# Attention and router block on one Trainium2 core: zero products ahead of the first weights' products, the first four weight combinations in four PSUM banks, and a new order of the opening

## The chip, the cores and the metric

One core of a Trainium2 chip. The metric is the time on the device in microseconds (us), the median of several runs of one launch.

## What is computed

```python
x = hidden_states                                    # (4, 512, 512), fp32
mod = (silu(c) @ wmod).reshape(4, 6, 1, 512)         # sa, ca, ga, sb, cb, gb
h = layernorm(x) * (1 + ca) + sa
# attention: 32 heads of 128, 8 kv heads, causal
q = rope(h @ Wq.T)
k = concat(h @ Wdk.T @ Wupk.T, rope(h @ Wkr.T))      # 64 + 64 of the 128 columns
v = h @ Wdk.T @ Wupv.T
x = x + ga * (softmax(q k.T / sqrt(128)) @ v @ Wo.T)
h = layernorm(x) * (1 + cb) + sb
# router: softmax over 64 experts, top 8, weighted bias rows
x = x + gb * (h * sum(top8) + top8_weights @ expert_bias)
```

The gates ga and gb are kept at least 0.25 from zero.

## The kernel before, in words

Every matrix is split into a high part in fp32r and a low part (the value less the high part), and each product is three: high by high, high by low, low by high (`passes`). The main loop `step(t)` goes over 128 heads (8 kv groups, 4 batches, 4 heads of a group); ahead of it stands an opening of some 100 us, whose order on each engine is written out by hand. Engines meet through counting semaphores.

The opening has these pieces. The names in brackets are helpers of the engines' programs:

- **Combined weights.** Wup times Wdk, once for all batches: `combine(i)`, i from 0 to 15, on PE (L606 to L614). i // 4 is one of four pieces of Wup, i % 4 a slice of 128 columns of Wdk. A combination is 12 products of 384 columns, into the bank of COMBINE_BANKS. ACT copies each to wc_out and counts act_comb (L1063), SP stores it to HBM. The first needs the split of wup (ACT L1060, DVE L1459) and of wdk in four pieces (ACT L1054, DVE L1454).
- **Modulation.** `modulation(j)`, j = 0 and 1: 16 fp32 products from c_silu and wmod (L566), transposed by `transpose_modulation` (L580) in bank pv and copied by DVE to modT.
- **h.** For batch b: DVE's `statistics`, POOL's `statistics` (rstd and shift_x), ACT's `normalise_x(b)` (four instructions on y, L1072), PE's `transpose_h(n)` (4 transposes; n // 4 is the batch), DVE's `modulate_h(n)`, ACT's `split_h(n)` and POOL's `split_h(n)` for high and low part. transpose_h(n) waits for act_xn, normalise_x of its batch.
- **First weights.** SP's `load_first(i)` brings wq0, wk, wq1, wv, wq2, wq3 in turn into two stage buffers; ACT's `split_first(i)` makes the high part, POOL's `split_piece` the low one. wk comes in two loads, of which the second reads the stored combinations back, so SP waits there until the first four are stored.
- **Heads.** `k_proj(0)`, `q_proj(t)` (12 products of 512 columns each), then DVE's and POOL's rope (rot_c, rot_s, kv_rot), ACT's and POOL's `q_split` and `k_split`, and `scores(t)`. q_proj(t) for t under 5 writes bank pv and waits until DVE's `q_rope(t - 1)` (L1467 to L1469) has read the one before. DVE's q_rope(t) waits for POOL's q_split(t - 1), because rot_c is one buffer.

The order on PE: combinations 0, 1, 2, modulation 0, combination 3, modulation 1, transpose_h 0 and 1, transpose_modulation, and so on (L903 to L940). SP has one queue for all loads and stores.

```python
def transpose_h(n):
    b, c = n // CH, n % CH
    pe.wait_ge(act_xn, b + 1)
...
def q_proj(t):
...
    elif t > 0:
        pe.wait_ge(dve_r, t)
```

## Time and profile before

| what | us |
|---|---|
| median of 3 runs | 1451.87 (1451.16 to 1452.57) |
| the profiled execution | 1451.52 |
| its span, first to last instruction | 1450.2 |
| PE busy | 1430.0 (99%) |
| DVE, ACT, POOL busy | 1152.9, 1009.4, 1023.5 |
| PE's first product | at 9.28 |

The page gives shares over the whole span. For the opening one reads the timeline, which lists the instructions of each engine by start, with the idle time before and what ended it. The ends of matmuls are modelled, so their distance from start to start says more than their duration. The span leaves out 1.3 us that lie around it.

### The profile page before, as it was taken

How to read it: one execution, taken by the hardware profiler on the slowest of the kernel's cores; microseconds unless marked ns; L12 is line 12 of the kernel's file. 1: busy time of each engine (PE TensorE's matmuls, PEld its weight loads, DVE VectorE, ACT ScalarE, POOL GpSimd, SP SyncE). 2: the span in 40 equal slices, each digit the busy share in tenths (PEclk: the TensorE clock that was granted, in tenths of full speed). 3: DMA queues.
4: the chain of work that ended last, by engine and by line, in shares of the span. 5: the costliest groups of instructions: out<-in, count | busy, mean ns of one | idle time of the engine just before them, and what ended most of it. 6: DMA issues, size and time to landing. Idle time of an engine off the chain costs nothing.

```text
span 1450.2 us, 24714 instructions
## 1 busy us (share of the span) xinstructions
PE 1430.0 (99%) x7150; PEld 1209.0 (83%) x7150; DVE 1152.9 (79%) x3542; ACT 1009.4 (70%) x2391; POOL 1023.5 (71%) x805
## 2 busy tenths in 40 slices
PE   7999999999999999999999999999999999999998
PEld 7888888888888888888888888888888888888886
DVE  6697777777777777778777777777879989888876
ACT  5687767667767667676777677676667676776674
POOL 3777777667767666776666677667588887887662
PEclk9999999999999999999999999999999999999999
DMA  9488658766766866686588668659888889888972
GB/s 316 157 248 255 213 179 229 221 213 184 213 202 199 228 197 214 191 244 180 172 229 241 203 180 227 181 176 259 241 229 267 264 284 272 277 256 271 269 234 68
DMA packets 215158, 322.05 MB, mean 222 GB/s; under 512 B 42512, under 2 KB 132464, under 8 KB 215024
## 3 DMA queue, kind: packets, MB, share of 16 engines
q1 hardware_dynamic: 214736, 320.39, 74.2%
q8 instruction: 59, 0.97, 0.3%
q14 instruction: 75, 0.61, 0.1%
q10 hardware_dynamic: 288, 0.07, 0.0%
HBM read 179.43 MB, written 140.95 MB: 221 GB/s over the span
## 4 chain that ended last, share of the span: by engine, by line
PE 90%; DVE 4%; DMA 2%; issue 1%; POOL 1%; ACT 1%; SPq 0%; DVEq 0%; ACTq 0%
PE bank_s L642 22%; PE bank_o L804 22%; PE bank_pv L766 14%; PE bank_s L708 13%; PE bank_s L674 6%; PE bank_s L659 5%; PE bank_s L613 2%; DMA PT_raw<-blocks 1%; PE bank_pv L642 1%; PE bank_s L704 1%; PE bank_o L613 1%; POOL PT_lo L1891 1%; PE bank_s L868 1%; DVE blocks L1529 0%; DMA blocks<-blocks 0%
## 5 line engine op out<-in xcount | busy, mean ns | idle before, releaser
L1891 POOL TENSOR_TENSOR PT_lo<-PT_raw,PT_hi 128x640 fp32r<-128x640 f32 x246 | 382.7, 1577 | 30.7 <-ACT PT_hi L1152 30.7
L1138 ACT ACTIVATE probs<-probs,row_inv 128x512 f32<-128x512 f32 (+3 forms) x512 | 257.7, 553 | 193.7 <-DVE row_inv L1512 193.6
L1879 POOL TENSOR_TENSOR rot_c<-rot_c,rot_s 128x512 f32<-128x512 f32 x128 | 167.9, 1312 | 251.7 <-DVE rot_s L1469 251.7
L1131 ACT ACTIVATE probs<-probs,row_min 128x384 f32<-128x384 f32 (+3 forms) x512 | 281.6, 552 | 47.2 <-DVE row_min L1505 47.1
L1529 DVE STREAM_TRANSPOSE blocks<-probs 128x384 f32<-128x384 f32 x508 | 213.9, 447 | 19.7 <-ACT probs L1138 13.5
L708 PE MATMUL bank_s<-kT_both,qT_hi 128*128 128x512 f32 (+2 forms) x768 | 215.5, 341 | 1.8 <-issue 1.1
L1505 DVE CUSTOM_DVE_ANT_0 probs<-bank_s,mask 128x512 f32<-128x512 f32 (+2 forms) x384 | 205.3, 552 | 0.3
L1884 POOL TENSOR_TENSOR qT_lo<-rot_c,qT_hi 128x512 fp32r<-128x512 f32 x128 | 166.3, 1299 | 51.4 <-ACT qT_hi L1113 50.6
L804 PE MATMUL bank_o<-wo_lo,OT_hi 128*128 128x512 f32 x496 | 195.0, 393 | 0.4 <-DVE rot_s L1469 0.4
L804 PE MATMUL bank_o<-wo_hi,OT_hi 128*128 128x512 f32 x496 | 193.4, 390 | 0.0
L642 PE MATMUL bank_s<-hT_lo,wq_hi 128*128 128x512 f32 x480 | 193.0, 402 | 0.4
L804 PE MATMUL bank_o<-wo_hi,OT_lo 128*128 128x512 f32 x496 | 193.0, 389 | 0.0
L642 PE MATMUL bank_s<-hT_hi,wq_hi 128*128 128x512 f32 x480 | 188.5, 393 | 0.0
L642 PE MATMUL bank_s<-hT_hi,wq_lo 128*128 128x512 f32 x480 | 187.4, 390 | 0.0
L1152 ACT ACTIVATE PT_hi<-PT_raw 128x640 fp32r<-128x640 f32 x250 | 169.9, 728 | 17.3 <-DMA PT_raw<-blocks 17.2
L708 PEld LDWEIGHTS bank_s<-kT_both,qT_hi 128*128 128x128 f32 x768 | 142.5, 188 | 19.3 <-issue 3.1
L1467 DVE TENSOR_TENSOR rot_c<-bank_s,cos_t 128x512 f32<-128x512 f32 x120 | 82.8, 690 | 81.0 <-PE bank_s L642 80.2
L1545 DVE TENSOR_TENSOR OT_lo<-bank_pv,OT_hi 128x512 fp32r<-128x512 f32 x123 | 84.6, 688 | 78.5 <-ACT OT_hi L1162 78.5
L766 PE MATMUL bank_pv<-PT_lo,v_hi 128*128 128x512 f32 x372 | 135.3, 369 | 1.3 <-DVE OT_lo L1545 0.8
L766 PE MATMUL bank_pv<-PT_hi,v_lo 128*128 128x512 f32 x372 | 132.5, 356 | 0.3 <-DVE OT_lo L1545 0.3
L766 PE MATMUL bank_pv<-PT_hi,v_hi 128*128 128x512 f32 x372 | 132.0, 356 | 0.0
L708 PE MATMUL bank_s<-kT_both,qT_lo 128*128 128x512 f32 (+2 forms) x384 | 129.2, 337 | 0.0
(311 smaller groups left out, 3198.0 us busy)
## 6 DMA issues: line engine op xcount, KB each, us to landing
blocks<-blocks SPq DMA_DIRECT2D x127, 640.0 KB, 3.6
PT_raw<-blocks SPq DMA_DIRECT2D x500, 160.0 KB, 3.9
stage<-in_wq SPq DMA_DIRECT2D x32, 256.0 KB, 5.2
vblocks<-kv_raw SPq DMA_DIRECT2D x32, 256.0 KB, 5.4
kv_raw<-vblocks SPq DMA_DIRECT2D x128, 64.0 KB, 2.2
stage<-in_wo SPq DMA_DIRECT2D x32, 256.0 KB, 5.1
split_wq<-wq_hi SPq DMA_DIRECT2D x32, 256.0 KB, 5.4
split_wq<-wq_lo SPq DMA_DIRECT2D x32, 256.0 KB, 5.8
```

The source lines that it names most:

```text
L642: mm = pe.matmul(q_bank(t)[:], w[:, h, c, :], x[:, b * CH + c, :], start=(c == 0 and n == 0), stop=(c == CH - 1 and n == 2))
L708: mm = pe.matmul(score_bank[qt], q, k[:, 0:keys], start=(n == 0), stop=(n == 2))
L766: mm = pe.matmul(to[:, :, (first - tiles[0]) * SUB:], v_part[:, kb, :], ps[:, :, at:at + size], start=(start and kb == 0 and n == which[0] ...
L804: mm = pe.matmul(bank[f"o{j}"][:], o[:, o_at:o_at + P], w[:, h, :], start=(u < LAST_UNIT and h == 0 and n == 0), stop=(u < LAST_UNIT - 1 a ...
L1131: ins = act.activation(row(t, qt), row(t, qt), ACT.Exp, bias=row_min[m][:, qt:qt + 1], scale=-1.0, accum_out=row_sum[m][:, qt:qt + 1])
L1138: ins = act.activation(row(t, qt), row(t, qt), ACT.Copy, scale=row_inv[t % 2][:, qt:qt + 1])
L1152: act.activation(parts_of(t)[0][:, at], raw_of(t)[:, at], ACT.Copy).then_inc(act_t, 1)
L1505: dve.tensor_tensor_reduce(row(t, qt), score_bank[qt], row(t, 0) if qt == 0 else mask[:, SEQ - (qt + 1) * P:], -SCALE, -LOWEST, ALU.add, A ...
L1529: ins = dve.transpose(blocks_v[:, qt:qt + 3 * whole_keys - 2:3], keys[:, 0:whole_keys])
L1879: pool.tensor_tensor(rot_c[:], rot_c[:], rot_s[:], ALU.add).then_inc(pool_a, 1)
L1884: pool.tensor_tensor(lo[:], rot_c[:], hi[:].bitcast(F32), ALU.subtract).then_inc(pool_q, 1)
L1891: pool.tensor_tensor(lo[:, at], raw_of(t)[:, at], hi[:, at].bitcast(F32), ALU.subtract).then_inc(pool_t, 1)
```

## The change

1. **Zero products.** WARM_UPS = 13 fp32 products of 128 columns from kv_rot, into bank s1, where nobody reads them. DVE clears kv_rot as its first instruction for that (before, it did so ahead of the split).
2. **Splits piece by piece.** wup's first piece is split in four pieces in turn with wdk's four (`split_first_weights` on ACT and DVE), in place of one whole wup and four of wdk.
3. **Side by side.** `combine_first` makes combinations 0 to 3 together in banks s3, s2, pv and o3: for each of the four pieces, first the four products of high by high, then the 32 with a low part, one combination after the other. The number of products is the same. transpose_modulation and k_proj(0) wait for ACT's copies out of pv and o3.
4. **Order.** On PE, modulation 0 follows combination 3, and the later combinations move among the transposes; combination 10 goes from behind transpose_h(7) to ahead of k_proj(0). On ACT, normalise_x(0) goes behind combinations 2 and 3, and normalise_x(1) behind split_first(1). On POOL, split_h(1) goes ahead of statistics(1) and k_split(0) ahead of split_h(6). On DVE, modulate_h(1) goes ahead of statistics(1). On SP, the load of wmod[1] goes ahead of the first store.

```diff
-COMBINE_BANKS = ["s3", "s2"] * (SOON // 2) + ["o0", "o1"] * ((COMBINED - SOON) // 2)
+SIDE_BY_SIDE = ["s3", "s2", "pv", "o3"]
+COMBINE_BANKS = SIDE_BY_SIDE + ["s3", "s2"] * ((SOON - CH) // 2) + ["o0", "o1"] * ((COMBINED - SOON) // 2)
+WARM_UPS = 13
...
-        SILU, POWER, ROT_CLEAR, HALF, MODT = 5, 6, 7, 8, 9
+        ROT_CLEAR, SILU, POWER, HALF, MODT = 1, 6, 7, 8, 9
...
                 pe.wait_ge(d_ident, 16)
+                pe.wait_ge(act_comb, SIDE_BY_SIDE.index("pv") + 1)
...
+            def warm_up():
+
+                pe.wait_ge(dve_pro, ROT_CLEAR)
+                for _ in range(WARM_UPS):
+                    pe.matmul(bank["s1"][:, 0:P], kv_rot[:, 0:P], kv_rot[:, P:2 * P], start=True, stop=True)
+
+            def combine_first():
+
+                for m in range(CH):
+                    pe.wait_ge(split_w, 2 * m + 2)
+                    for i in range(CH):
+                        pe.matmul(bank[COMBINE_BANKS[i]][:, 0:2 * KVC], wdk[0][:, m, i * P:(i + 1) * P],
+                                  wup_hi[0][:, m, :], start=(m == 0), stop=False)
+                for i in range(CH):
+                    for m in range(CH):
+                        if i == 0:
+                            pe.wait_ge(split_lo, 2 * m + 2)
+                        for k, (down, up) in enumerate(((wdk[0], wup_lo[0]), (wdk[1], wup_hi[0]))):
+                            mm = pe.matmul(bank[COMBINE_BANKS[i]][:, 0:2 * KVC], down[:, m, i * P:(i + 1) * P],
+                                           up[:, m, :], start=False, stop=(m == CH - 1 and k == 1))
+                    mm.then_inc(pe_comb, 1)
+
             def combine(i):
                 n, c = i // CH, i % CH
                 ps = bank[COMBINE_BANKS[i]]
                 if c == 0:
-                    pe.wait_ge(split_lo, n + 1 + (CH if n > 0 else 0))
-                if i >= 2:
-                    pe.wait_ge(act_comb, i - 1)
+                    pe.wait_ge(split_lo, n + 2 * CH)
+                pe.wait_ge(act_comb, i - 3 if i < CH + 2 else i - 1)
                 for m in range(CH):
-                    if i == 0:
-                        pe.wait_ge(split_lo, m + 2)
...
-            combine(0)
-            combine(1)
-            combine(2)
+            warm_up()
+            combine_first()
             modulation(0)
-            combine(3)
+            combine(4)
             modulation(1)
             transpose_h(0)
             transpose_h(1)
             transpose_modulation()
-            combine(4)
             combine(5)
             transpose_h(2)
             combine(6)
             transpose_h(3)
             combine(7)
             combine(8)
+            combine(9)
             transpose_h(4)
             transpose_h(5)
-            combine(9)
+            combine(10)
             pe.wait_ge(pool_h, CH)
+            pe.wait_ge(act_comb, SIDE_BY_SIDE.index("o3") + 1)
             k_proj(0)
             transpose_h(6)
             pe.wait_ge(pool_h, CH)
             pe.wait_ge(dve_pro, MODT)
             q_proj(0)
             transpose_h(7)
-            combine(10)
             q_proj(1)
             combine(11)
...
-            def split_down():
+            def split_first_weights():
+                act.wait_ge(d_wup[0], 16)
                 for m in range(CH):
+                    act.activation(wup_hi[0][:, m, :], wup_in[0][:, m, :], ACT.Copy).then_inc(split_w, 1)
                     act.wait_ge(d_wdk[m], 16)
...
-            split_up(0)
-            split_down()
+            split_first_weights()
             combine(0)
             split_up(1)
             combine(1)
-            normalise_x(0)
             combine(2)
             combine(3)
+            normalise_x(0)
+            combine(4)
             split_h(0)
-            combine(4)
+            split_h(1)
             split_up(2)
+            combine(5)
             split_first(0)
-            combine(5)
-            split_h(1)
+            combine(6)
             split_h(2)
-            combine(6)
-            normalise_x(1)
             split_h(3)
             combine(7)
             split_first(1)
+            normalise_x(1)
             combine(8)
             split_first(2)
             split_h(4)
             combine(9)
             split_h(5)
+            combine(10)
             normalise_x(2)
             split_up(3)
+            k_split(0)
             split_h(6)
-            k_split(0)
             split_first(3)
+            q_split(0)
             split_first(4)
-            combine(10)
-            q_split(0)
             split_h(7)
+            q_split(1)
             combine(11)
-            q_split(1)
...
-            def split_down():
+            def split_first_weights():
                 for m in range(CH):
-                    dve.wait_ge(split_w, m + 2)
+                    dve.wait_ge(split_w, 2 * m + 1)
+                    dve.tensor_tensor(wup_lo[0][:, m, :], wup_in[0][:, m, :], wup_hi[0][:, m, :].bitcast(F32),
+                                      ALU.subtract).then_inc(split_lo, 1)
+                    dve.wait_ge(split_w, 2 * m + 2)
...
+            dve.memset(kv_rot[:], 0.0).then_inc(dve_pro, 1)
             dve.memset(c_silu[:], 0.0).then_inc(dve_pro, 1)
             dve.wait_ge(act_pro, 1)
             dve.tensor_scalar(c_exp[:], c_exp[:], 1.0, None, ALU.add).then_inc(dve_pro, 1)
-            dve.wait_ge(dve_pro, 2)
+            dve.wait_ge(dve_pro, 3)
             dve.reciprocal(c_exp[:], c_exp[:]).then_inc(dve_pro, 1)
-            dve.wait_ge(dve_pro, 3)
+            dve.wait_ge(dve_pro, 4)
             dve.tensor_tensor(c_keep[:], c_in[:], c_exp[:], ALU.mult).then_inc(dve_pro, 1)
-            dve.wait_ge(dve_pro, 4)
+            dve.wait_ge(dve_pro, 5)
             dve.tensor_copy(c_silu[:, :, 0:BATCH], c_keep[:]).then_inc(dve_pro, 1)
             dve.memset(power[:], -0.5).then_inc(dve_pro, 1)
-            dve.memset(kv_rot[:], 0.0).then_inc(dve_pro, 1)
             dve.memset(minus_half[:], -0.5).then_inc(dve_pro, 1)
-            split_up(0)
-            split_down()
+            split_first_weights()
             statistics(0)
             split_up(1)
             keep_modulation(0)
             keep_modulation(1)
             transpose_modulation()
             modulate_h(0)
+            modulate_h(1)
             statistics(1)
-            modulate_h(1)
...
             statistics(0)
             split_h(0)
+            split_h(1)
             statistics(1)
             split_piece(FIRST_CHUNKS[0], 0, 0)
-            split_h(1)
             split_h(2)
             split_h(3)
             split_piece(FIRST_CHUNKS[1], 1, 1)
...
             split_h(4)
             split_h(5)
             k_rope(0)
+            k_split(0)
             split_h(6)
             q_rope(0)
-            k_split(0)
...
+            sp.dma_start(wmod[1][:], wmod_v[MOD_PIECES[1]]).then_inc(d_wmod[1], 16)
             store_combined(0)
-            sp.dma_start(wmod[1][:], wmod_v[MOD_PIECES[1]]).then_inc(d_wmod[1], 16)
```

ACT from its first exponential on: before, and then after. The names are wup and wdk (weights to combine) and wc_out (a combination's copy).

```order
L1271 ACTIVATE c_exp<-c_in 128x16
L1060 ACTIVATE wup_hi_171<-wup_in_173 128x1536
L1054 ACTIVATE wdk_hi<-wdk_in 128x512 x4
L1066 ACTIVATE wc_out_177<-bank_s 128x384
L1060 ACTIVATE wup_hi_172<-wup_in_175 128x1536
```

```order
L1294 ACTIVATE c_exp<-c_in 128x16
L1075 ACTIVATE wup_hi_171<-wup_in_173 128x384
L1077 ACTIVATE wdk_hi<-wdk_in 128x512
L1075 ACTIVATE wup_hi_171<-wup_in_173 128x384
L1077 ACTIVATE wdk_hi<-wdk_in 128x512
L1075 ACTIVATE wup_hi_171<-wup_in_173 128x384
```

The one long split of wup became four, each followed by a piece of wdk; the last two pairs stand below the rows shown.

ACT between the copy of combination 6 and the second piece of wq, before and after. `y<-y` is normalise_x(1), `wk_hi` is split_first(1), `hT_hi` is split_h.

```order
L1066 ACTIVATE wc_out_178<-bank_s 128x384
L1079 ACTIVATE hT_hi<-h_raw 128x512 x2
L1066 ACTIVATE wc_out_179<-bank_s 128x384
L1072 ACTIVATE y<-y,shift_x,rstd 128x512 x4
L1079 ACTIVATE hT_hi<-h_raw 128x512
L1066 ACTIVATE wc_out_180<-bank_s 128x384
L1092 ACTIVATE wk_hi<-stage_58 128x512
L1066 ACTIVATE wc_out_177<-bank_s 128x384
```

```order
L1089 ACTIVATE wc_out_179<-bank_s 128x384
L1102 ACTIVATE hT_hi<-h_raw 128x512 x2
L1089 ACTIVATE wc_out_180<-bank_s 128x384
L1115 ACTIVATE wk_hi<-stage_58 128x512
L1095 ACTIVATE y<-y,shift_x,rstd 128x512 x4
L1089 ACTIVATE wc_out_177<-bank_s 128x384
L1115 ACTIVATE wq_hi<-stage_57 128x512
L1102 ACTIVATE hT_hi<-h_raw 128x512
```

The four instructions on y stood ahead of wk_hi and now stand behind it.

PE from the end of q_proj(0) to the start of what follows transpose_h(7), before and after. `bank_pv` is a head's projection, `ident,y` a transpose.

```order
L642 MATMUL bank_pv<-hT_hi,wq_lo 128x512
L642 MATMUL bank_pv<-hT_hi,wq_hi 128x512
L599 MATMUL bank_o<-ident,y 128x128 x4
L613 MATMUL bank_o<-wup_lo_174,wdk_hi 128x384
L613 MATMUL bank_o<-wup_hi_171,wdk_lo 128x384
L613 MATMUL bank_o<-wup_hi_171,wdk_hi 128x384
```

```order
L664 MATMUL bank_pv<-hT_hi,wq_lo 128x512
L664 MATMUL bank_pv<-hT_hi,wq_hi 128x512
L602 MATMUL bank_o<-ident,y 128x128 x4
L664 MATMUL bank_pv<-hT_lo,wq_hi 128x512
L664 MATMUL bank_pv<-hT_hi,wq_lo 128x512
L664 MATMUL bank_pv<-hT_hi,wq_hi 128x512
```

Combination 10 (its rows with wup and wdk) stood between transpose_h(7) and q_proj(1), and is gone from there.

## Rows read from the trace of the kernel before

**Rows 1.** The page's table of engines: busy us, share of the span, instructions.
```profile
PE 1430.0 (99%) x7150; PEld 1209.0 (83%) x7150; DVE 1152.9 (79%) x3542; ACT 1009.4 (70%) x2391; POOL 1023.5 (71%) x805
```

**Rows 2.** Timeline, PE, 9 to 22: start us, us, line, tile, [idle before <-releaser].
```profile
9.28 0.66 PE L613 MATMUL bank_s<-wup_lo,wdk_hi 128*128 128x384 f32 x1 [9.28 <-DVE wdk_lo L1454]
...
13.57 0.33 PE L613 MATMUL bank_s<-wup_hi,wdk_lo 128*128 128x384 f32 x1
...
17.68 1.08 PE L566 MATMUL bank_o<-wmod,c_silu 128*32 128x128 f32 x32
...
20.99 1.08 PE L566 MATMUL bank_o<-wmod,c_silu 128*32 128x128 f32 x32
...
22.00 0.66 PE L599 MATMUL bank_s<-ident,y 128*128 128x128 f32 x4
```

**Rows 3.** Timeline, PE, at 1436: the fp32 products, and the next group.
```profile
1435.88 1.06 PE L884 MATMUL bank_o<-diagonal,h2T_end 128*128 128x128 f32 x8
1436.70 0.48 PE L892 MATMUL bank_o<-experts_lo,weightT 128*128 128x512 f32 x1
```

**Rows 4.** Timeline, ACT: the splits of the weights and batch 0's normalising.
```profile
5.27 1.47 ACT L1060 ACTIVATE wup_hi<-wup_in 128x1536 fp32r<-128x1536 f32 x1
6.64 2.17 ACT L1054 ACTIVATE wdk_hi<-wdk_in 128x512 fp32r<-128x512 f32 x4
...
13.88 1.48 ACT L1060 ACTIVATE wup_hi<-wup_in 128x1536 fp32r<-128x1536 f32 x1
...
17.24 2.93 ACT L1072 ACTIVATE y<-y,shift_x,rstd 128x512 f32<-128x512 f32 x4 [1.05 <-POOL shift_x L1865]
```

**Rows 5.** Timeline, DVE: low parts, statistics, and q_rope(0).
```profile
8.44 2.49 DVE L1454 TENSOR_TENSOR wdk_lo<-wdk_in,wdk_hi 128x512 fp32r<-128x512 f32 x4
...
11.13 2.47 DVE L1436 BATCH_NORM_STATS2 stats<-y 128x6 f32<-128x512 f32 x4 [0.19 <-DMA y<-in_x]
...
43.73 0.69 DVE L1467 TENSOR_TENSOR rot_c<-bank_pv,cos_t 128x512 f32<-128x512 f32 x1 [0.26 <-PE bank_pv L642]
...
45.14 0.68 DVE L1469 TENSOR_TENSOR rot_s<-bank_pv,sin_t 64x512 f32<-64x512 f32 x1
```

**Rows 6.** Timeline, PE, 34 to 58: transpose_h(4), k_proj(0), q_proj(1), scores(0), scores(1).
```profile
34.50 0.60 PE L599 MATMUL bank_s<-ident,y 128*128 128x128 f32 x4
...
37.48 0.39 PE L659 MATMUL bank_o<-hT_lo,wk_hi 128*128 128x512 f32 x1
...
46.01 0.40 PE L642 MATMUL bank_pv<-hT_lo,wq_hi 128*128 128x512 f32 x1
...
50.84 0.39 PE L708 MATMUL bank_s<-kT_both,qT_hi 128*128 128x512 f32 x1
...
57.54 0.50 PE L708 MATMUL bank_s<-kT_both,qT_hi 128*128 128x512 f32 x1
```

**Rows 7.** Timeline, POOL: qT_lo(0), rot_c(1), qT_lo(1).
```profile
48.40 1.32 POOL L1884 TENSOR_TENSOR qT_lo<-rot_c,qT_hi 128x512 fp32r<-128x512 f32 x1
...
52.15 2.83 POOL L1879 TENSOR_TENSOR rot_c<-rot_c,rot_s 128x512 f32<-128x512 f32 x1
...
56.19 1.29 POOL L1884 TENSOR_TENSOR qT_lo<-rot_c,qT_hi 128x512 fp32r<-128x512 f32 x1
```

**Rows 8.** DMA: windows (busy us PE to POOL, PEclk, DMA share, GB/s); issues; us to landing.
```profile
10.00:15.00 5.00, 5.00 (x21) 5.00 (x21) 3.79 (x10) 1.51 (x2) 0.73 (x3) 1.00 0.96 379
15.00:20.00 5.00, 5.00 (x55) 4.55 (x54) 2.05 (x2) 3.61 (x6) 2.13 (x2) 1.00 0.98 297
...
4.13 1.95 SPq L2253 DMA_DIRECT2D wmod<-in_wmod  x4
...
30.23 0.66 SPq L2132 DMA_DIRECT2D stage<-wc_scratch  x1
...
wmod<-in_wmod SPq DMA_DIRECT2D x4, 256.0 KB, 9.8
...
stage<-wc_scratch SPq DMA_DIRECT2D x1, 128.0 KB, 3.2
```

More of the change, by code:

```diff
@@ L1457, in split_up @@
             def split_up(n):
-                dve.wait_ge(split_w, n + 1 + (CH if n > 0 else 0))
+                dve.wait_ge(split_w, n + 2 * CH)
                 dve.tensor_tensor(wup_lo[n % 2][:], wup_in[n % 2][:], wup_hi[n % 2][:].bitcast(F32),
```

## The prediction

> **What bounds the kernel now.** First the page's table of engines: TensorE (PE) is busy for 99% of the span [rows 1], so the end moves with PE. Then PE in order of time. Its first product waits 9.28 us for a DVE subtraction; the products then come 0.33 us apart, and from 13.57 us on 0.175 us apart (23 of them fill 13.57 to 17.68) [rows 2]. So the first 13 ran at half rate, the level of 1.2 GHz, and the rest at 2.4. The column of the granted clock says 1.00 for 10:15 too [rows 8], where most of the slow ones lie, so the spacing is my evidence. From there to 57.54 no row of PE carries a wait over 0.3 us. But "PE is full" is not "only PE is full": at 57.54 the reader is to see PE released by POOL to within 0.1 us, since POOL's qT_lo ends at 56.19 + 1.29 = 57.48 [rows 6, 7], and POOL is dense from 48.40 up to it. And DMA moves 379 and 297 GB/s in the stretches 10:15 and 15:20 [rows 8], of its share 96 and 98%. Three things thus run nearly level in the first 58 us, and a lead of one is worth only what the others follow.
>
> **The first four combinations.** Before: PE has combinations 0 to 3 and the first modulation behind it at 20.99 [rows 2]. After:
> - 13 zero products. The nearest fp32 products of 128 columns: 8 records (4 products) from 1435.88 to 1436.70, 0.21 us each at the full level [rows 3], so 0.42 at half. They start when DVE has cleared kv_rot, first on its queue now, about 1.4. If the level rises 4.3 us after the first product, as from 9.28 to 13.57, ten run slowly and three fast: end 6.3. If it doesn't rise, 1.4 + 13 x 0.42 = 6.9.
> - ACT: pieces of 384 and 512 columns in turn. A full wup takes 1.47, a 512 piece 0.54 [rows 4]; a 384 piece is about 0.4, so 0.94 a pair; from 5.27 the pairs end at 6.3, 7.3, 8.2 and 9.2. 0.2 more than now; DVE and PE cover it.
> - DVE: 0.47 + 0.62 a pair [rows 5], from 6.35 (the memset is gone from there) to 10.7.
> - PE: four high products per pair, the last four 9.2 to 9.9; then 32 more at 0.175. The last low piece (10.7) is there when it is its turn (9.9 + 6 x 0.175 = 10.95). End 15.5. Modulation 0 needs wmod0, four loads issued from 4.13 to 6.08 and landing 9.8 later, so the last about 15.6 [rows 8]; it ends at 16.5.
> So 16.5 stands against 20.99: **a lead of 4.5 us on PE.** If zero products raised no clock, the level would rise 4.3 us after 6.3: 13 products at 0.33, and 15.5 becomes about 16.7.
>
> **What the lead meets.** Combination 4 needs the split of wup1: ACT's 1.48 from 13.88 at the latest [rows 4], then three times DVE's 0.62, 17.2 at worst. So it ends between 18.7 and 19.3, and modulation 1 by 20.3. The transposes of batch 0 need normalise_x(0), and that hangs on x, DVE's statistics at 11.13 and POOL, as now: it ends at 17.24 + 2.93 = 20.2 [rows 4, 5]. They start at 20.2, not at 22.00. A combination is 12 x 0.175 = 2.1; transpose_h(4), (5) and combination 9 take 34.50 to 37.48 [rows 6], so a transpose_h 0.44. From 20.2: transposes 0 and 1 and the modulation's 1.2, combinations 5 to 9 10.5, transposes 2 and 3 0.9, makes 32.8; with short waits for copies PE stands before transpose_h(4) at about 33.0: before, at 34.50 with combination 9 (2.1) still to do, 36.6. Lead 3.6.
>
> *First loss.* ACT's new order has split_first(1), the high part of wk, ahead of normalise_x(1); before, normalise_x(1) came first. wk's second load goes out at 30.23 and takes 3.2, so wk is there at 33.4 [rows 8]. It is behind the same bytes as now in one queue. What can come forward is the thin stretch 15:20: (379 - 297) x 5 us = 0.41 MB, at 379 GB/s 1.1 us, which the earlier issue of wmod1 fills; I take 1.2, so 32.2. ACT then needs 0.54 + 2.93: transpose_h(4) at 35.6, and PE waits **2.6 us** for it. Combination 10 (its bank o0 is free) is now ahead of k_proj(0): 35.6 + 0.9 + 2.1 = 38.6, where before k_proj starts at 37.48 [rows 6] without it (39.6 with it). Lead 1.0.
>
> *Second loss.* Combination 10 stood between transpose_h(7) and q_proj(1). q_proj(1) writes bank pv, which DVE's q_rope(0) must have read. A projection is 46.01 to 50.84 [rows 6] less a combination, 2.75. So k_proj to 41.35, transpose_h(6) to 41.75, q_proj(0) to 44.5, transpose_h(7) to 44.9; q_rope(0) starts at 44.8 and takes 2.1 (43.73 to 45.14 + 0.68 [rows 5]), to 46.9. Before, combination 10 filled that time and q_proj(1) began at 46.01; now 46.95, a wait of **2.0 us**. q_proj(1) to 49.7, combination 11 to 51.8: scores(0) at 51.8 against 50.84 [rows 6]. The lead is a lag of 1.0.
>
> *POOL.* DVE's k_rope after k_proj ends at 43.8. POOL: add 45.05, (ACT 0.6) kT_lo 46.95, hT_lo 48.2, rot_c 49.5, (ACT 0.6) qT_lo 51.4, each 1.25 to 1.3; before, qT_lo ended at 48.40 + 1.32 [rows 7]. Then wv 52.65 and wq2 53.9. scores(0) is 50.84 to 57.54 less a projection and a combination, 1.85, so PE is at q_proj(2) at 53.65 and waits 0.3; q_proj(2) to 56.8, combination 12 to 58.9. scores(1) there, against 57.54: lag 1.4. POOL's rot_c from 53.9 is the open price: 1.3 as its neighbours, or 2.83 as at 52.15 [rows 7], where DVE ran its wup_lo subtraction. DVE's order around it is unchanged, so I take 2.83: 56.7, hT_lo 58.0, qT_lo 59.3. Lag 1.85. The Trainium skill (SBUF — State Buffer, SBUF: two separate sides) says that a DVE instruction with two SBUF inputs and a GpSimd one hold a shared port pair exclusively. By that rule the long price returns wherever the pair overlaps, lag 1.85; by the neighbours' row alone it would be 1.4. The 2.83 of row 7 agrees with the rule.
>
> After scores(1) the order is the old one, and of PE's 20.2 us without a product 9.28 are its start, so I see no long wait that would absorb a lag; it stays. Sum, against the profiled execution: 1451.5 + 1.4 to 1.85, middle 1.6: 1453.1. The median of the runs is 0.35 above that execution: **1453.5 us**. The earlier wmod1, the wc_out banks pv and o3 and their two new waits on ACT's copies cost nothing: those copies end by 16.0, before the modulation's transposes. The removed memset and reordered POOL splits lie in POOL's idle stretch.
>
> **Rivals.** A measurement of this kernel can tell about 0.2% (2.9 us) from no change.
> - *A, the above:* both waits, 1453.5; 0.55. By its own bounds 1452.9 to 1454.3.
> - *B, wk is early:* its load lands before ACT's copy of combination 7, at about 30.4, and the first wait goes; PE, then DVE and POOL come 2.6 sooner, and 1.6 - 2.6 = -1.0: 1450.9. Against it: the queue's bytes, 1.8 us more than the thin stretch gives. 0.10.
> - *C, the lead carries:* neither wait is there and PE keeps the 3.6 us of transpose_h(4): 1448.3. For it: no row shows either wait yet. Against it: POOL ended level with PE at 57.5, and would have to come forward too. 0.15.
> - *D, the clock falls:* PE idles 2.6 us at transpose_h(4) and again 2.0 at q_proj(1); if the level drops there, the next 4.3 us at half rate do the work of 2.15 us (as 9.28 to 13.57), so 1453.5 + 2.15 = 1455.7. It decides once the first wait is as long as I have it. Against it: I know no stretch of this trace with such a gap. 0.15. The Trainium skill (TensorE: Matmul & The Clock Gate, HAM oscillation) holds that idle gaps between bursts can put the array back to 1.2 GHz; it speaks against the change as ordered here.
> - *E, the zero products raise nothing:* first combinations end 1.2 later; the wait at transpose_h(4) swallows it, and the time is A's. 0.05.
>
> **How the numbers follow.** Faster by over 0.2% (under 1449.0) is C: 0.15. Slower by over 0.2% (over 1454.8) is D: 0.15. A, B and E lie within: 0.70. The range leaves out C alone: 1449.0 to 1456.5, the upper end D with A's upper bound.
>
> **What would show it.** PE at full rate from before 7 us; combinations 0 to 3 done by 15.5; batch 0's transposes at 20.2; transpose_h(4) at 35.6 behind ACT's normalise, with ACT idle ahead of wk_hi; q_proj(1) released by DVE rot_s near 47; scores(1) between 58.9 and 59.4 with POOL's qT_lo just ahead. Wrong if transpose_h(4) starts under 34, if q_proj(1) has no wait, or if products after either are 0.33 us apart.

## The result, and the profile after

The changed kernel 1456.36 us (median of 8 runs, 1454.37 to 1459.06), the kernel before 1452.22 us (8 runs, 1451.16 to 1453.57). The ratio is 1.0029, 95% interval 1.0019 to 1.0038: **slower by 4.1 us**. A second series of the same kernel gave 1.0034 (1.0021 to 1.0046). The time lies in the range, 0.14 us below its upper end, where the case was *D, the clock falls*, not A. The profiled execution of the change took 1458.79 us, among the two slowest of the eight.

The page of the changed kernel, table of engines and span: the work is the old one, with 26 records more on PE for the 13 zero products and three more each on DVE and ACT for the smaller pieces (against [rows 1]). So the loss is idle time or slow time.

```profile
span 1457.5 us, 24771 instructions
PE 1438.0 (99%) x7176; PEld 1215.1 (83%) x7176; DVE 1152.1 (79%) x3545; ACT 1010.6 (69%) x2394; POOL 1023.8 (70%) x805
```

Timeline of PE in the changed kernel to 21 us, against [rows 2] (start, duration, line, tile; in brackets the idle time before and its releaser):

```profile
1.44 5.51 PE L609 MATMUL bank_s<-kv_rot 128*128 128x128 f32 x26 [1.44 <-DVE kv_rot L1743]
6.70 0.59 PE L616 MATMUL bank_s<-wup_hi,wdk_hi 128*128 128x384 f32 x2
...
15.73 0.34 PE L623 MATMUL bank_o<-wup_hi,wdk_lo 128*128 128x384 f32 x1
16.00 1.08 PE L568 MATMUL bank_o<-wmod,c_silu 128*32 128x128 f32 x32
```

The opening did what it should: the first weights' products start at 6.70 us and come 0.17 to 0.18 us apart wherever they don't wait for the next split piece, combinations 0 to 3 end at 15.9, and combination 4 and the second modulation follow (19.31 to 20.3). At 20.50 us PE starts transpose_h(0); before it was 22.00 [rows 2]. The lead is lost behind that. The two longest waits of PE in the first 70 us of the changed kernel, by the view of waits:

```profile
PE bank_s L602 <- ACT y L1095: 2.7, 1, 2.7
PE bank_pv L664 <- DVE rot_s L1494: 1.8, 1, 1.8
```

and its timeline, against [rows 6]:

```profile
33.15 0.34 PE L635 MATMUL bank_s<-wup_hi,wdk_hi 128*128 128x384 f32 x1
36.21 0.66 PE L602 MATMUL bank_s<-ident,y 128*128 128x128 f32 x4 [2.72 <-ACT y L1095]
...
37.50 0.52 PE L635 MATMUL bank_o<-wup_hi,wdk_lo 128*128 128x384 f32 x1
37.82 0.52 PE L635 MATMUL bank_o<-wup_hi,wdk_hi 128*128 128x384 f32 x1
...
40.80 0.39 PE L681 MATMUL bank_o<-hT_lo,wk_hi 128*128 128x512 f32 x1
...
49.20 0.50 PE L664 MATMUL bank_pv<-hT_lo,wq_hi 128*128 128x512 f32 x1 [1.82 <-DVE rot_s L1494]
...
51.49 0.63 PE L664 MATMUL bank_pv<-hT_hi,wq_hi 128*128 128x512 f32 x1
51.92 0.63 PE L664 MATMUL bank_pv<-hT_lo,wq_hi 128*128 128x512 f32 x1
...
55.74 0.39 PE L730 MATMUL bank_s<-kT_both,qT_hi 128*128 128x512 f32 x1
...
62.43 0.39 PE L730 MATMUL bank_s<-kT_both,qT_hi 128*128 128x512 f32 x1
```

The reader is to see two things. Both waits of the prediction are there. And behind the first, combination 10's products stand 0.32 us apart, not 0.175: half rate. Behind the second, q_proj(1)'s products are 0.23 us apart until 50.69, and only then 0.43: the slow rows begin 1.5 us after PE has resumed. scores(1) starts at 62.43 against 57.54, a lag of 4.9. The windows of the changed kernel tell the same by the granted clock (window; its length, busy us of PE, PEld, DVE, ACT, POOL; then PEclk, DMA share, GB/s). It is 0.71 and 0.66 right behind the two waits; before, the column said 1.00 in all of them, of which two are shown below.

```profile
30.00:35.00 5.00, 3.49 (x21) 3.17 (x19) 2.85 (x8) 2.91 (x6) 4.99 (x5) 1.00 0.83 236
35.00:40.00 5.00, 3.79 (x17) 3.79 (x18) 1.53 (x2) 3.57 (x7) 4.52 (x7) 0.71 0.98 296
...
45.00:50.00 5.00, 3.18 (x17) 2.43 (x15) 4.63 (x8) 2.64 (x4) 3.23 (x3) 1.00 0.03 9
50.00:55.00 5.00, 5.00 (x18) 4.29 (x17) 3.79 (x10) 1.67 (x3) 4.26 (x4) 0.66 0.00 0
```

The kernel before:

```profile
35.00:40.00 5.00, 5.00 (x28) 4.55 (x27) 1.53 (x2) 2.87 (x6) 4.67 (x8) 1.00 1.00 340
50.00:55.00 5.00, 5.00 (x28) 4.42 (x27) 4.94 (x12) 0.49 (x1) 5.00 (x4) 1.00 0.49 131
```

ACT in the changed kernel holds a third wait, which the prediction does not have:

```profile
32.70 0.63 ACT L1115 ACTIVATE wk_hi<-stage 128x512 fp32r<-128x512 f32 x1 [2.09 <-DMA stage<-wc_scratch]
33.24 2.92 ACT L1095 ACTIVATE y<-y,shift_x,rstd 128x512 f32<-128x512 f32 x4
...
41.28 0.49 ACT L1089 ACTIVATE wc_out<-bank_o 128x384 f32<-128x384 f32 x1 [2.01 <-DMA wc_scratch<-wc_out]
41.67 2.93 ACT L1095 ACTIVATE y<-y,shift_x,rstd 128x512 f32<-128x512 f32 x4
44.50 1.47 ACT L1083 ACTIVATE wup_hi<-wup_in 128x1536 fp32r<-128x1536 f32 x1
47.34 0.63 ACT L1142 ACTIVATE kT_both<-kv_raw 128x512 fp32r<-128x512 f32 x1 [1.37 <-POOL kv_raw L1920]
```

The first row is the one expected: ACT stands 2.09 us for wk, with normalise_x(1) behind it. The row at 41.28 is ACT's copy of combination 10. There are four wc_out buffers, so it waits until the store of combination 6 has landed (that store was issued at 35.60), and normalise_x(2), split_up(3) and k_split(0) stand behind it. Before, this copy came at 47.22, when nothing held it. In the changed kernel nobody waits for it in turn: ACT is through with what stands behind the copy at 45.97 and then stands 1.37 us for POOL's kv_raw, ahead of k_split(0) (row at 47.34). POOL's chain to the scores starts with that kv_raw, which waits for DVE's rope of k_proj(0), and so for PE:

```profile
46.03 1.28 POOL L1920 TENSOR_TENSOR kv_raw<-kv_raw,kv_rot 128x512 f32<-128x512 f32 x1 [5.04 <-DVE kv_rot L1503]
...
52.55 1.29 POOL L1908 TENSOR_TENSOR qT_lo<-rot_c,qT_hi 128x512 fp32r<-128x512 f32 x1 [0.74 <-ACT qT_hi L1136]
```

Before, these two stood at 42.71 and, in [rows 7], at 48.40. So kv_raw is 3.3 us late, as k_proj(0) is (40.80 against 37.48), and qT_lo(0) 4.15. The other 0.85 us comes with POOL's new order: with k_split(0) ahead of split_h(6), POOL stands 0.74 us for ACT at k_split(0) and again at q_split(0), where it had other work before.

### The profile page after: what moved, and what is told of

It reads as the page before. It is cut to its first block, busy times and chain, and to the rows that moved or that the text cites. A ratio compares the mean times of both kernels' runs of the same rounds, so it can differ in the third digit from the quotient of the medians.

```text
span 1457.5 us, 24771 instructions
## 1 busy us (share of the span) xinstructions
PE 1438.0 (99%) x7176; PEld 1215.1 (83%) x7176; DVE 1152.1 (79%) x3545; ACT 1010.6 (69%) x2394; POOL 1023.8 (70%) x805
## 4 chain that ended last, share of the span: by engine, by line
PE 88%; DVE 4%; DMA 3%; ACT 2%; issue 2%; SPq 1%; POOL 0%; DVEq 0%; ACTq 0%
PE bank_s L664 22%; PE bank_o L826 22%; PE bank_pv L788 14%; PE bank_s L730 13%; PE bank_s L696 5%; PE bank_s L681 5%; DMA PT_raw<-blocks 1%; PE bank_s L726 1%; PE bank_pv L664 1%; PE bank_o L635 1%; DMA wc_scratch<-wc_out 1%; PE bank_s L890 1%; DVE blocks L1554 1%; SPq L2219 1%; DMA blocks<-blocks 1%
```

## The experiments

All times are medians; they come from several chips, so kernels are compared by the ratio, which is to the kernel before on the same chip. The waits, the lowest granted clock of a 5 us window from 30 to 60 us, and the start of scores(1) come from one profiled execution each. A fall is a stretch in which the clock is granted at its lower level. The expectations of the first four kernels name 61.6 us for scores(1) in the changed kernel. That is the end of GpSimd's half of q (1); TensorE's product starts at 62.43.

| kernel | us | ratio (95%) | wait ahead of transpose_h(4) | of q_proj(1) | clock | scores(1) |
|---|---|---|---|---|---|---|
| the change | 1456.36 | 1.0029 (1.0019, 1.0038) | 2.7 | 1.8 | 0.66 | 62.43 |
| after_again | 1457.31 | 1.0034 (1.0021, 1.0046) | 3.0 | 1.8 | 0.66 | 62.89 |
| fill_waits | 1454.96 | 1.0009 (1.0000, 1.0018) | filled | filled | 1.00 | 60.25 |
| norm_first | 1453.93 | 1.0008 (0.9999, 1.0017) | none | 1.8 | 0.66 | 60.26 |
| comb10_back | 1454.72 | 1.0014 (1.0005, 1.0022) | 2.8 | none | 0.66 | 59.93 |
| copy_later | 1452.35 | 1.0005 (0.9997, 1.0014) | none | 1.8 | 1.00 | 57.34 |
| both_moved | 1452.57 | 1.0000 (0.9991, 1.0009) | none | none | 1.00 | 56.88 |
| no_zeros | 1456.37 | 1.0028 (1.0018, 1.0039) | 1.3 | 1.8 | 0.78 | 60.08 |
| old_order | 1451.49 | 0.9988 (0.9979, 0.9997) | none | none | 1.00 | 56.87 |
| old_no_zeros | 1452.05 | 0.9997 (0.9988, 1.0006) | none | none | 1.00 | 56.39 |
| q_split_early | 1451.39 | 0.9992 (0.9983, 1.0001) | none | none | 1.00 | 57.52 |
| q_early_no_zeros | 1451.12 | 0.9994 (0.9985, 1.0002) | none | none | 1.00 | 56.14 |
| split_before_rope | 1452.88 | 1.0005 (0.9996, 1.0014) | none | none | 0.66 | 59.96 |

From scores(1) on a single execution varies: what is left of the span behind it was 1391.8 to 1395.9 us over these profiles. So scores(1) tells the mechanism, and the ratio, over several runs, the price.

### fill_waits: is it the standing still that lowers the clock?

```diff
+            def keep_busy(n, bank_name):
+                for _ in range(n):
+                    pe.matmul(bank[bank_name][:, 0:P], ident[:], ident[:], start=True, stop=True)
             combine(9)
+            keep_busy(12, "o0")
             transpose_h(4)
...
             transpose_h(7)
+            pe.wait_ge(act_comb, 11)
+            keep_busy(8, "o0")
             q_proj(1)
```

> The changed kernel with products that nobody reads in both of TensorE's waits: twelve fp32 products of the identity with itself into bank o0 ahead of transpose_h(4), eight ahead of q_proj(1) (at 0.21 us each 2.5 and 1.7 us). The clock theory: the granted clock fell in the changed kernel (0.71 at 35 to 40 us, 0.66 at 50 to 55) because TensorE had stood still for 2.7 and 1.8 us before. With the products it stays at 1.00 in both stretches; transpose_h(4) still starts at about 36.2 us, since its release comes from ScalarE, but q_proj(1) starts 1.5 to 2 us earlier, scores(1) at 58.5 to 59.5 instead of 61.6, and the time falls by 2 to 4 us below the changed kernel's, to the one of my case A, 1452.5 to 1454.5. The rival, that the waits by themselves or what lies behind them on ScalarE and GpSimd cost the time: the clock is at 1.00 but scores(1) stays within 0.5 us of 61.6 and the time within 1 us of the changed kernel's. A second rival, that the clock falls for another reason than the standing still: it is under 0.9 in these stretches again, and the time is no shorter.

PE in fill_waits:

```profile
33.33 2.84 PE L614 MATMUL bank_o<-ident 128*128 128x128 f32 x24
36.30 0.66 PE L602 MATMUL bank_s<-ident,y 128*128 128x128 f32 x4
...
37.41 0.34 PE L640 MATMUL bank_o<-wup_hi,wdk_lo 128*128 128x384 f32 x1
...
39.35 0.39 PE L686 MATMUL bank_o<-hT_lo,wk_hi 128*128 128x512 f32 x1
...
47.75 0.50 PE L669 MATMUL bank_pv<-hT_lo,wq_hi 128*128 128x512 f32 x1
...
52.73 0.42 PE L735 MATMUL bank_s<-kT_both,qT_hi 128*128 128x512 f32 x1
```

transpose_h(4) starts no sooner (36.30 against 36.21), but combination 10 runs at full rate, and from transpose_h(4) to k_proj(0) it is 3.05 us, not 4.59. From q_proj(1) to scores(0) it is 4.98, not 6.54. So **each fall costs 1.55 us**, and filling both is worth 0.0020 of the time, 2.9 us: work that nobody reads makes the kernel faster. The fall is not the releaser's doing, since the releases stayed. scores(1), at 60.25, was 0.75 us later than the latest I had given, and 2.7 us later than the 57.54 of before. POOL in fill_waits says what sets it:

```profile
44.58 1.29 POOL L1928 TENSOR_TENSOR kv_raw<-kv_raw,kv_rot 128x512 f32<-128x512 f32 x1 [3.48 <-DVE kv_rot L1511]
46.60 1.28 POOL L1932 TENSOR_TENSOR kT_both<-kv_raw,kT_both 128x512 fp32r<-128x512 f32 x1 [0.74 <-ACT kT_both L1150]
...
51.13 1.30 POOL L1916 TENSOR_TENSOR qT_lo<-rot_c,qT_hi 128x512 fp32r<-128x512 f32 x1 [0.74 <-ACT qT_hi L1144]
```

k_proj(0), at 39.35, is 1.9 us later than before, and kv_raw with it; POOL's new order adds 0.85, and qT_lo(0) is 2.7 us late. scores(1) follows POOL.

### norm_first and comb10_back: one wait at a time

```diff
             combine(7)
-            split_first(1)
             normalise_x(1)
+            split_first(1)
             combine(8)
```

> The changed kernel with ScalarE's normalise_x(1) ahead of split_first(1), so that it does not stand behind the 0.63 us split whose input landed at 32.2 us. The theory that this split's DMA makes transpose_h(4) late: normalise_x(1) starts at 30 to 31 us instead of 33.2, transpose_h(4) runs right behind the products of combination 9 at 33.2 to 33.8 us with under 0.5 us of waiting, and the granted clock stays at 1.00 from 35 to 40 us. The second wait, for q_rope(0) on VectorE, remains, and with it the fall behind 50 us. Time 1.5 to 4 us below the changed kernel's. The rival, that the first wait is swallowed by what comes later (ScalarE's copy of combination 10, held by a store, and VectorE's and GpSimd's chains behind 41 us): TensorE's start of q_proj(1) stays at 49 to 49.5 us, scores(1) at 61 to 62 us, and the time within 1 us of the changed kernel's.

transpose_h(4) runs right behind combination 9 (33.43 us), with no fall behind it, and k_proj(0) starts at 36.41, 4.4 us sooner than in the change. The time falls by 0.0021 of it, 3.0 us, within what was expected. But scores(1) is at 60.26, the same as in fill_waits. PE has now a wait for POOL ahead of scores(0):

```profile
44.80 0.50 PE L664 MATMUL bank_pv<-hT_lo,wq_hi 128*128 128x512 f32 x1 [1.82 <-DVE rot_s L1494]
...
52.72 0.47 PE L730 MATMUL bank_s<-kT_both,qT_hi 128*128 128x512 f32 x1 [1.20 <-POOL qT_lo L1908]
```

and ACT and POOL of norm_first say why: the copy of combination 10 is where it was, at 41.39, though PE is 4.4 us sooner. It now holds k_split(0), and POOL stands 3.73 us for that. That scores(1) is the same as in fill_waits is a coincidence of two different chains.

```profile
41.39 0.49 ACT L1089 ACTIVATE wc_out<-bank_o 128x384 f32<-128x384 f32 x1 [3.57 <-DMA wc_scratch<-wc_out]
...
46.67 1.29 POOL L1924 TENSOR_TENSOR kT_both<-kv_raw,kT_both 128x512 fp32r<-128x512 f32 x1 [3.73 <-ACT kT_both L1142]
```

```diff
-            combine(10)
             pe.wait_ge(act_comb, SIDE_BY_SIDE.index("o3") + 1)
             k_proj(0)
...
             transpose_h(7)
+            combine(10)
             q_proj(1)
```

comb10_back is this edit on PE, and on ACT the copy of combination 10 behind q_split(0).

> The changed kernel with combination 10 back between transpose_h(7) and q_proj(1) on TensorE, and its copy on ScalarE back behind q_split(0). The first wait (2.7 us, transpose_h(4)) and its fall of the clock stay. The theory that the moved combination opened the second wait: k_proj(0) and q_proj(0) start some 3 us earlier (37.5 to 38.5 and 40.5 to 42 us), q_proj(1) waits under 0.3 us, the granted clock from 50 to 55 us is over 0.95, scores(1) starts 2 to 4 us earlier than 61.6, and the time is 2 to 4 us below the changed kernel's. The rival, that the second wait is only the sum of what VectorE has to do for q_rope(0) and comes back elsewhere: q_proj(1) or scores(0) waits as much as before, and the time stays within 1 us of the changed kernel's.

The second wait is gone, and with it the second fall (1.00 from 40 to 60 us; the clock fell once more near the end of this execution, 0.66 at 1425 to 1430 us). scores(1) comes at 59.93, 2.5 us sooner, and the ratio falls by 0.0015, 2.2 us, though the two intervals overlap. The first wait is there, and the clock is 0.66 behind it, which now hits k_proj(0).

### copy_later: the third wait

On norm_first, ACT's copy of combination 10 is moved behind q_split(0); PE is as in norm_first.

```diff
             split_h(5)
-            combine(10)
             normalise_x(2)
...
             q_split(0)
+            combine(10)
             split_first(4)
```

> norm_first once more, with ScalarE's copy of combination 10 moved behind q_split(0); on TensorE combination 10 stays ahead of k_proj(0). In norm_first this copy stood 3.6 us for the store of combination 6, and normalise_x(2), split_up(3) and k_split(0) stood behind it; GpSimd then had 3.7 us of nothing before its half of k. The theory that this copy is a third wait of the change, on ScalarE: normalise_x(2) starts at 37.8 to 38.5 us, k_split(0) at 42 to 43, GpSimd's half of q (0) at 47.5 to 48.5 instead of 51.17, scores(0) at 50 to 51 although q_proj(1) still waits some 1.8 us for VectorE and its products still run under a fallen clock (q_proj(1) ends at 48.8, combination 11 at 51), and scores(1) at 57.5 to 58.5 instead of 60.26. Ratio 0.999 to 1.001 against 1.0008 of norm_first. The rival, that q_proj(1)'s wait and the fallen clock set the rest: scores(1) stays at 59.8 to 60.5 us and the ratio within 0.0005 of norm_first's.

PE's order and its wait of 1.82 us are those of norm_first, yet scores(0) starts at 49.82 instead of 52.72 and scores(1) at 57.34 instead of 60.26. ACT's normalise_x(2) starts at 38.12 instead of 41.77, and POOL's chain comes forward as a whole:

```profile
43.68 1.27 POOL L1924 TENSOR_TENSOR kT_both<-kv_raw,kT_both 128x512 fp32r<-128x512 f32 x1 [0.74 <-ACT kT_both L1142]
...
48.20 1.29 POOL L1908 TENSOR_TENSOR qT_lo<-rot_c,qT_hi 128x512 fp32r<-128x512 f32 x1 [0.74 <-ACT qT_hi L1136]
```

scores(1) gained 2.9 us; the ratio fell by 0.0003 only, which the intervals don't tell from nothing. By the ratio the rival holds as well. Two of the expectation's numbers failed: scores(0) and scores(1) came sooner than I had them. The clock did not fall behind the 1.8 us this time (1.00 in the window 45:50), so part of the 2.9 us may be the fall that was missing, and not the copy.

### both_moved: are the two places all of it?

norm_first and comb10_back together.

> Both repairs together: normalise_x(1) ahead of split_first(1) on ScalarE, and combination 10 back between transpose_h(7) and q_proj(1) with its copy behind q_split(0). The theory that these two places hold all that the change lost: neither wait is left, the granted clock is 1.00 in every stretch to 60 us, and, since comb10_back with the first wait and a slow stretch of 3 us still in it reached scores(1) at 59.93 us, that one now starts at 56.5 to 57.5 us (57.54 in the kernel before). Time 1450.5 to 1452.5 us, ratio to the kernel before 0.998 to 1.0005. The rival, that the remainder of the spreading (combination 4 between the halves of the modulation, both halves of modulate_h ahead of statistics(1)) costs by itself: scores(1) at 58 us or later and a ratio of 1.001 or more.

No wait over 0.9 us is left (0.86 for POOL's wk_lo ahead of k_proj(0) is new), the clock is 1.00 throughout, scores(1) at 56.88 as expected, and the ratio 1.0000. **What the change loses lies, to within 1.3 us, in these two places of the order.** Against copy_later only combination 10's place on PE differs: scores(1) at 56.88 against 57.34, and ratios that the intervals don't tell apart. What the second wait costs by itself, where the clock holds and ACT's copy is out of the way, was thus not measurable.

### no_zeros, old_order, old_no_zeros, q_split_early and its twin: what the first parts are worth

no_zeros is the change with this edit:

```diff
-WARM_UPS = 13
+WARM_UPS = 0
```

> The changed kernel without the thirteen zero products, nothing else. The theory of my prediction, that they are swallowed by the wait for y ahead of transpose_h(4): the first combinations end 1 to 2 us later, the wait ahead of transpose_h(4) is shorter by what TensorE comes later (2.7 down to 1 to 2 us), transpose_h(4) starts within 0.5 us of 36.2, and with less time standing still the granted clock may hold there. Ratio 1.001 to 1.003, no slower than the changed kernel's 1.0029. The rival, that the zero products carry through: transpose_h(4) over 1 us later than 36.2 and a ratio of 1.0035 or more.

PE in no_zeros:

```profile
7.55 0.52 PE L616 MATMUL bank_pv<-wup_hi,wdk_hi 128*128 128x384 f32 x1
7.87 0.52 PE L616 MATMUL bank_o<-wup_hi,wdk_hi 128*128 128x384 f32 x1
...
16.89 1.08 PE L568 MATMUL bank_o<-wmod,c_silu 128*32 128x128 f32 x32
...
35.39 0.66 PE L602 MATMUL bank_s<-ident,y 128*128 128x128 f32 x4 [1.33 <-ACT y L1095]
```

Without the zero products the first eleven or so real ones are 0.32 us apart, and modulation 0 comes 0.9 us later. The time is the same, 1.0028 against 1.0029: the wait ahead of transpose_h(4) was 1.3 us instead of 2.7. That transpose came 0.8 us sooner than in the change, since wk landed sooner in this execution (ACT's split of it began at 31.89, not at 32.70); I had given it 0.5. Behind 1.3 us of standing still the clock held. One thing does not fit: with one fall instead of two, scores(1) is 2.35 us sooner than in the change (60.08), and norm_first, with as late a scores(1), has 1.0008. What took that lead away behind scores(1) was not settled, so scores(1) alone doesn't give the price.

old_order keeps the change up to modulation 0 and has everything behind it in the order before, on PE, ACT, DVE and POOL; SP still loads wmod[1] ahead of the first store. Its edit on PE begins:

```diff
             warm_up()
             combine_first()
             modulation(0)
-            combine(4)
             modulation(1)
             transpose_h(0)
...
```

> The parts of the change that lie ahead of 17 us alone (thirteen zero products, the first weights split piece by piece, four combinations side by side), and everything behind them in the order of the kernel before, on TensorE, ScalarE, VectorE and GpSimd. The theory that the first three parts gain and the spreading loses: the first combinations end at 15.5 to 16 us, no wait of over 1 us stands ahead of transpose_h(4) or q_proj(1), the granted clock stays at 1.00 to 60 us, and a lead of 0.5 to 2 us is kept to scores(1) (55.5 to 57 us instead of 57.5): time 0.5 to 2 us below the kernel before, 1450 to 1451.7. The rival, that the early lead is given back by the loads that the later combinations wait for (they land when they land): scores(1) at 57.3 to 57.8 us and a time within 0.5 us of the kernel before. Should it be slower than the kernel before by over 1 us, the loss lies in the first three parts and not in the spreading.

transpose_h(4) starts at 32.71 (34.50 before), k_proj(0) at 35.69 (37.48), scores(1) at 56.87 (57.54): of 1.8 us of lead 0.7 reach scores(1). With **0.9988 (0.9979 to 0.9997), 1.7 us faster,** it is the one kernel here whose interval lies below the kernel before.

> old_order (ratio 0.9988) without the thirteen zero products. The theory that they raise TensorE's clock before the first real product comes: without them the first products run at half rate for some 3 to 5 us of work, a combination 1 to 2 us later each, modulation(0)'s first half at 17 to 18 us instead of about 16. Since the second half of the modulation waited 1.3 us for wmod in old_order, most of the loss is swallowed there; transpose_h(0) 0 to 0.7 us later, ratio 0.9988 to 0.9995. The rival, that they are worth the whole of old_order's gain: ratio 0.9995 or more and transpose_h(4) at 34 us or later instead of 32.71.

Modulation 0 at 16.83 instead of 15.8, transpose_h(0) at 20.64 instead of 20.20, both behind ACT's y, scores(1) at 56.39. The ratio, 0.9997, is above the 0.9988 to 0.9995 expected and would suit the rival, whose transpose_h(4) at 34 us did not come (33.13); the intervals don't tell it from old_order's.

q_split_early takes ACT's q_split(0) ahead of the copy of combination 10 and of split_first(4) in old_order; q_early_no_zeros is the same without the zero products.

```diff
             split_first(3)
+            q_split(0)
-            split_first(4)
             combine(10)
-            q_split(0)
+            split_first(4)
```

> old_order (ratio 0.9988) with one more edit on ScalarE: q_split(0) directly behind split_first(3), ahead of combination 10's copy and of split_first(4), whose input landed at 46.15 us; GpSimd stood 0.92 us for q_split(0) there. The theory that GpSimd's chain from its half of q (0) to its half of q (1) sets scores(1): that half starts at 46.8 to 47.1 us instead of 47.76, scores(1) at 56.0 to 56.3 instead of 56.87, ratio 0.9975 to 0.9990. The rival, that TensorE's own products set it: scores(1) stays at 56.7 to 57.0 and the ratio within 0.0005 of old_order's.

> q_split_early without the thirteen zero products. In old_no_zeros modulation(0) ran 1.0 us later than with them, but transpose_h(0) at the same 20.6 us, since both waited for y from ScalarE. The theory that the zero products are worth nothing at the end: scores(1) within 0.5 us of q_split_early's and the ratio within 0.0008 of its. The rival, that they are worth their 1.0 us: ratio larger than q_split_early's by 0.0007 or more.

(transpose_h(0) was at 20.20 in old_order, not at 20.6 as this text has it; in this pair it is at 20.57 and 20.59.)

The ratios are 0.9992 and 0.9994. So zero products made no difference that can be measured in three pairs (1.0029 and 1.0028; 0.9988 and 0.9997; 0.9992 and 0.9994). The four kernels with the early parts and the old order lie at 0.9993 on average, about 1 us faster; neither rival of q_split_early is settled, for its profile was disturbed by its own waits. PE stood 1.68 us for wmod and 0.91 for y, with 1 us of products between, and the clock fell (windows of q_split_early):

```profile
18.00:20.00 2.00, 1.08 (x32) 0.84 (x32) 0.28 (x1) 2.00 (x4) 0.00 (x0) 1.00 1.04 384
20.00:22.00 2.00, 1.43 (x7) 1.44 (x8) 0.01 (x1) 0.51 (x1) 0.00 (x0) 0.52 1.07 429
22.00:24.00 2.00, 2.00 (x11) 2.00 (x10) 0.89 (x2) 0.00 (x0) 0.00 (x0) 0.63 1.01 390
```

Its scores(1), 57.52, is late, as the fall adds to its waits; in the twin without the fall it is at 56.14, where the expectation of q_split_early had it, and so 1.4 us from q_split_early's, not within 0.5.

### after_again: is a fall chance?

> The changed kernel once more, unedited. Behind the same 1.8 us of waiting ahead of q_proj(1) the granted clock fell in the changed kernel (0.66), norm_first (0.66) and no_zeros (0.78), but not in copy_later (1.00). The theory that each fall is a matter of chance for the single execution, while the waits are fixed by the order: both waits are there again (2.5 to 2.9 us ahead of transpose_h(4), 1.8 ahead of q_proj(1)), the clock of 35 to 40 us or of 50 to 55 us differs from the first profile's 0.71 and 0.66 by over 0.1 in at least one, the profiled time differs from 1458.79 us accordingly, and the median lies at 1455 to 1457.5. The rival, that the falls are fixed like the waits: 0.71 and 0.66 within 0.05 again, profiled time 1458 to 1459.5.

The clock was 0.73 and 0.66 in the same two windows, the profiled time 1457.81, just under the rival's 1458. ACT's copy of combination 10 waited for no store here (it started at 41.47, released by PE), and scores(1), at 62.89, was no sooner for it. My theory that the falls differ from one execution to the next fell for this kernel: by this measure they repeat. Over the whole span the mean clock was 0.997 to 0.999 in all 13 runs of the change and 1.000 in 10 of 11 runs of fill_waits. Where only the 1.8 us wait is left, it does vary: norm_first had 1.000 in 6 of 11 runs, and copy_later's profile shows 1.00 behind it. The six runs of norm_first at 1.000 are no faster than its other five (means 1454.4 and 1454.1 us): there PE waits 1.2 us for POOL ahead of scores(0) in any case, so a fall ahead of it seems to cost nothing.

### split_before_rope: who slows GpSimd's rot_c

```diff
+            split_up(3)
             q_rope(1)
-            split_up(3)
             mask_and_max(0, 0)
```

> q_split_early with VectorE's split_up(3) (1.87 us) ahead of q_rope(1) instead of behind it. In every kernel so far GpSimd's rot_c for q (1), which ran beside that split, took 2.8 us against 1.3 for the same operation beside other work. The theory that two operations of two inputs in SBUF on VectorE and GpSimd get in each other's way: rot_c (1) now takes 1.3 us, and the GpSimd operation that lies beside the split instead takes 2.6 to 2.9 (its half of wv or of wq); q_rope(1) starts some 1.2 us later, scores(1) within 1 us of q_split_early's. The rival, that rot_c (1) is slow by itself (its inputs, its place behind the rope): 2.8 us again and its neighbours at 1.3.

POOL and DVE in split_before_rope:

```profile
48.47 1.29 POOL L1899 TENSOR_TENSOR wv_lo<-stage,wv_hi 128x512 fp32r<-128x512 f32 x1
49.72 2.79 POOL L1899 TENSOR_TENSOR wq_lo<-stage,wq_hi 128x512 fp32r<-128x512 f32 x1
53.45 1.29 POOL L1903 TENSOR_TENSOR rot_c<-rot_c,rot_s 128x512 f32<-128x512 f32 x1 [0.95 <-DVE rot_s L1494]
```

```profile
48.63 2.74 DVE L1484 TENSOR_TENSOR wup_lo<-wup_in,wup_hi 128x1536 fp32r<-128x1536 f32 x1
```

rot_c takes 1.29 now, and wq_lo, which lies beside the split, 2.79. The slowness goes with the overlap, not with the operation. The split itself takes 2.74 instead of 1.75 to 1.88; its start, 1.1 us before wv_lo ends, suggests that it stood for wv_lo, and wq_lo then for it. scores(1), 59.96, is 2.4 us later than q_split_early's, not 1: q_proj(2) waited 1.8 us for DVE's later q_rope(1), and the clock fell to 0.66 once more.

## Why the prediction was right and wrong

- **The opening: right.** Combinations 0 to 3 end at 15.9 (15.5 forecast), modulation 0 at 17.0 (16.5), batch 0's transposes start at 20.50 (20.2). The 0.3 is POOL's: rstd took 2.44 us beside DVE's split and shift_x 0.20, where before they took 1.05 and 1.34; I had taken y "as now". The zero products ended at 6.7, not 6.3: the starts of their records are 0.213 us apart up to 6.30 (two records a product, so 0.43 at half rate), and 0.11 behind it. So between eleven and twelve ran slowly, not ten.
- **First loss: right in place, 0.6 off.** 2.7 us for 2.6, transpose_h(4) at 36.2 for 35.6, because wk landed at 32.7 and not at 32.2.
- **Second loss: right.** 1.8 us for 2.0, released by DVE's rot_s, by the mechanism given; comb10_back closes it.
- **The chance of D: the step that failed.** The text had both waits, and priced the fall behind the first only, with a chance of 0.15 on the ground that no stretch of the trace had such a gap. A, at 0.55, took both waits at their length and the clock's fall at nothing. The clock fell behind both, in each of two profiles, 1.55 us each: 3.1 in place of the 2.15 for one. The Trainium skill (TensorE: Matmul & The Clock Gate, HAM oscillation) says that idle gaps between bursts can put the array back to 1.2 GHz, and the rows agree. With both waits in the forecast, the absence of a counterexample was no evidence against the fall; D deserved more than 0.15, and its price was two falls. The chance of 0.15 for slower by over 0.2% met a ratio of 1.0029. That the range held 1456.36 is in part luck: its upper end had one fall, at 2.15 us, and A's upper bound.
- **A wait missed, without harm: ACT's copy of combination 10.** The prediction followed this combination on PE and looked at its bank, and not at its copy's buffer. The copy waited 2.0 us for a store. In the changed kernel this held nobody. It counts once the first wait is gone: from norm_first to copy_later scores(1) comes 2.9 us sooner.
- **POOL's chain: right.** From k_proj(0) to the end of qT_lo(1) the forecast had 20.7 us (38.6 to 59.3); it took 20.8 (40.80 to 61.62). qT_lo(0) came 2.4 us later than forecast because k_proj(0) was 2.2 later.
- **The lag at scores(1): 4.9, not 1.85.** The 3.05 us more are 0.6 for wk, 1.6 for the first fall, which stood ahead of k_proj(0), and 0.8 by which PE, with the second wait and its fall, came behind POOL (62.43 against 61.62, where it was to be level). fill_waits agrees: without the falls 2.2 us of the lag go. The whole time grew by less, 4.1 us at the median, though the profiled execution is 7.3 us longer than that of before; what is given back or lost behind scores(1), and where, was not settled.
- **rot_c's price: right**, 2.82 us for 2.83. What the Trainium skill (SBUF — State Buffer, SBUF: two separate sides) says of a port pair held exclusively agrees with split_before_rope, where the long price, 2.79, moved to the neighbour.
- **Rivals.** B and C did not occur. E's statement that zero products raise nothing is wrong (0.32 us without, 0.175 with them), but that the time is the same without them holds (1.0028).

## What to carry to other kernels

A lead at the front of an in-order engine is worth what its next wait leaves of it: here 4.0 us of lead at 17 us (20.99 less 17.01) became a lag of 4.9 at 62, because one split was put ahead of a normalise and one combination away from the place where it covered a wait. When a forecast has TensorE standing still for as long as here (1.8 and 2.7 us), price the clock's fall with it, at each such place, and consider filler products, which gave back 2.9 of 4.1 us here. When a piece of work moves on one engine, follow all that it issues on the others, the copy's buffer and its store included. And when two kernels reach the same moment, look at what released it in each: scores(1) at 60.25 and 60.26 came from two different chains.

## What the runs showed of the hardware

- The granted clock fell to half after 2.7 to 3.0 us of standing still in three of three profiles (the change twice, comb10_back), after 1.8 us in five of six (the change twice, norm_first, no_zeros, split_before_rope; not in copy_later), not after 1.3 us alone (no_zeros), and once after 1.7 and 0.9 us close together (q_split_early; not after 1.3 and 0.9 in old_order). Near the end of comb10_back it fell at 1425.5 us after waits of 0.5 and 1.1 us between short pieces of work. So the length of the last wait alone does not decide it. Each of the two falls that fill_waits took away had cost 1.55 us of PE's time.
- Products of a cleared tile raise the clock: with them the first real products are at full rate at 6.7 us, without them (no_zeros) the products of the first 3.3 us run at half rate.
- DVE's subtraction for wup_lo and a two-input operation on POOL, all inputs in SBUF, do not run side by side: 2.8 us for 1.3 on POOL, and 2.74 for 1.76 on DVE. DVE's rope, with one input in PSUM, does not slow POOL: 1.30 us for hT_lo at 44.24 in the kernel before, beside rot_s (44.43 and 45.14, the latter in [rows 5]).
